# Cross-attention scores in four 32-row tiles of the array, with a new order of work on five engines

## What is computed

```python
q = (query @ Wq.T + bq).reshape(B, T, H, D).transpose(0, 2, 1, 3)
k = (key @ Wk.T + bk).reshape(B, S, H, D).transpose(0, 2, 1, 3)
v = (value @ Wv.T + bv).reshape(B, S, H, D).transpose(0, 2, 1, 3)
scores = jnp.einsum('bhtd,bhsd->bhts', q, k) * scale
scores = scores + attn_mask[None, None, :, :]
pad = key_padding_mask[:, None, None, :]
scores = jnp.where(pad, -jnp.inf, scores)
probs = jax.nn.softmax(scores, axis=-1)
out = jnp.einsum('bhts,bhsd->bhtd', probs, v)
out = out.transpose(0, 2, 1, 3).reshape(B, T, E)
return out @ Wo.T + bo
...
x = x + _L0_xattn_ref(_layernorm(x, axis=-1), ctx_1024, ctx_1024, ...)
```

## Time and profile before

| | |
|---|---|
| median of 3 runs | 3068.27 us (3065.03 to 3068.76) |
| profiled execution, its own time | 3058.43 us |
| its span | 3056.6 us |
| busy in the span: PE, PEld | 2634.9 us (86%), 2059.3 us (67%) |
| busy: DVE, ACT, POOL | 1635.3 us (54%), 1090.0 us (36%), 1049.3 us (34%) |
| mean granted TensorE clock | 0.886 of full speed |
| first cross-attention | from the start to about 850 us |

### The profile page before, as it was taken

One profiled execution on the slowest core, in us unless ns is written; L12 is line 12 of the kernel. 1 busy time (PEld: TensorE's weight loads), 2 busy tenths in 40 slices (PEclk: granted clock), 3 DMA queues, 4 the chain that ended last, 5 costly groups with the idle time before them and its releaser, 6 DMA issues. The chain is left out here.

```text
span 3056.6 us, 53637 instructions
## 1 busy us (share of the span) xinstructions
PE 2634.9 (86%) x15674; PEld 2059.3 (67%) x15687; DVE 1635.3 (54%) x5365; ACT 1090.0 (36%) x2422; POOL 1049.3 (34%) x1187
## 2 busy tenths in 40 slices
PE   4999999999969998529999999968879999957774
PEld 4999999999969997415555555546657888833332
DVE  3666666666646554652233333326555555557773
ACT  2555555555524442001112222211115555534442
POOL 3444555555300000227600000027744444313564
PEclk9999999999967776569999999985559999979996
DMA  3000000000070000135322222236640000000001
GB/s 136 22 21 21 21 21 21 21 21 21 1 262 1 0 0 10 52 131 192 137 68 76 77 77 77 78 125 221 225 147 1 0 0 0 0 28 1 1 0 55
DMA packets 110897, 180.88 MB, mean 59 GB/s; under 512 B 13665, under 2 KB 86370, under 8 KB 109410
## 3 DMA queue, kind: packets, MB, share of 16 engines
q1 hardware_dynamic: 75058, 114.79, 11.1%
q0 software_dynamic: 12288, 33.57, 3.0%
q10 hardware_dynamic: 23472, 31.54, 3.0%
HBM read 116.93 MB, written 62.91 MB: 59 GB/s over the span
## 5 line engine op out<-in xcount | busy, mean ns | idle before, releaser
L405 ACT ACTIVATE xa_prob<-xa_neg_s,xa_neg_max 128x256 f32<-128x256 f32 x512 | 232.9, 502 | 272.1 <-DVE xa_neg_max L298 272.1
L1618 PE MATMUL ex_ps_h<-moew_w,ex_xT 128*128 x576 | 286.2, 619 | 20.5 <-DVE ex_xT L1676 9.7
L254 POOL TENSOR_TENSOR xa_qz<-xa_q,g_head_mask 128x512 fp32r<-128x512 f32 x256 | 266.3, 1075 | 108.9 <-DVE xa_q L361 108.9
L298 DVE CUSTOM_DVE_ANT_0 xa_neg_s<-xa_ps_s,xa_mask 128x256 f32<-128x256 f32 x512 | 196.9, 422 | 174.8 <-PE xa_ps_s L445 173.9
L472 PEld LDWEIGHTS xa_ps_o<-xa_v,xa_probT 128*128 128x128 f32 x2048 | 259.4, 193 | 12.3 <-ACT xa_probT L412 3.9
L472 PE MATMUL xa_ps_o<-xa_v,xa_probT 128*128 128x34 f32 x2048 | 254.5, 269 | 1.7 <-ACT xa_probT L412 1.4
L445 PE MATMUL xa_ps_s<-xa_kT,xa_qz 128*128 128x256 f32 x1536 | 246.3, 296 | 1.8 <-POOL xa_qz L254 1.8
L1671 DVE TENSOR_TENSOR ex_g<-ex_act_g,ex_ps_h 128x256 f32<-128x256 f32 x144 | 60.7, 422 | 309.9 <-ACT ex_act_g L1651 309.9
L998 DVE CUSTOM_DVE_ANT_0 sa_neg_s<-sa_ps_s,sa_mask 128x128 f32<-128x128 f32 x512 | 117.8, 286 | 170.5 <-PE sa_ps_s L1114 170.1
L445 PEld LDWEIGHTS xa_ps_s<-xa_kT,xa_qz 128*128 128x128 f32 x1536 | 199.5, 190 | 2.0 <-issue 2.0
L412 ACT ACTIVATE xa_probT<-xa_ps_t 128x512 f32<-128x512 f32 x256 | 151.3, 591 | 138.9 <-PE xa_ps_t L456 138.7
(11 more groups left out here) (285 smaller groups left out, 5735.4 us busy)
## 6 DMA issues: line engine op xcount, KB each, us to landing
expert_rows<-sa_zero SPq DMA_DIRECT2D x12, 1536.0 KB, 14.5
ex_xg<-expert_rows SPq DMA_DIRECT2D x144, 128.0 KB, 2.0
expert_outs<-ex_y ACTq DMA_DIRECT2D x144, 128.0 KB, 1.7
xa_ctxT<-in_ctxT_dram SPq DMA_DIRECT2D x32, 512.0 KB, 3.4
xb_ctxT<-in_ctxT_dram SPq DMA_DIRECT2D x32, 512.0 KB, 4.9
xb_ctx_rows<-in_ctx_rows_dram SPq DMA_DIRECT2D x32, 512.0 KB, 3.6
moew_w<-in_moe_w_dram ACTq DMA_DIRECT2D x8, 1024.0 KB, 5.5
g_x<-in_x_dram SPq DMA_DIRECT2D x4, 1024.0 KB, 9.9
```

Source lines behind the costliest of these rows:

```text
L254: ins = nc.gpsimd.tensor_tensor(qz[:, pp, part, g, b, :].rearrange("p (h t) -> p h t", h=HG), q2[:, pp, part, g, b * T:(b + 1) * T].unsque ...
L298: ins = nc.vector.tensor_tensor_reduce(neg_s[:, u % 2, i, :], ps_s[u % 2][:, i * S:(i + 1) * S], mask[:, u // 4, :], -1.0, 3e38, ALU.add, ...
L405: ins = nc.scalar.activation(prob[:, u % 2, i, :], neg_s[:, u % 2, i, :], ACT.Exp, bias=neg_max[:, u % 2, i:i + 1], scale=-1.0)
L1618: mm = nc.tensor.matmul(ps_h[1 - par][:, :], xT[:, 1 - par, k, :], c.w1[:, own, k, :], start=(k == 0), stop=(k == KC - 1))
```

## The change

The scores of one batch are computed at once instead of in four units. A head pair has 32 rows of `q` and `k`, so the array is used as four tiles of 32 rows, one for each bank of `ps_s`, which has four banks now; `qz` needs only to keep the two heads of a pair apart (`in_pair`) and is half as large, four instructions of 128x256. The transposes go back into the banks of the scores. The mask is made on GpSimd, from a `pad` that is loaded tile by tile. The rounded keys are made on ACT (`high_keys`). And the order of the work in a step changes on PE, DVE, ACT and GpSimd.

```diff
-        pad = ph.sb("pad", [P, B, S], U8)
+        pad = ph.sb("pad", [P, 2, 2, S], U8)
...
-        ps_s = [ph.ps(f"s{i}") for i in range(2)]
-        ps_t = [ph.ps(f"t{i}") for i in range(2)]
+        ps_s = [ph.ps(f"s{j}") for j in range(4)]
...
-            sp.dma_start(pad[:, :, :], d["pad"].to_broadcast([P, B, S])).then_inc(mask_loaded, 16)
...
-                    wait(sp, ctx_low, s - 1)
+                    wait(sp, pad_ready, s - 1)
                     sp.dma_start(ctxT[:, par, :, :], d["ctxT"][s, :, :, :]).then_inc(ctx_loaded[par], 16)
+                    sp.dma_start(pad[:, par, :, :], d["pad"][s, :, :, :].to_broadcast([P, 2, S]))\
+                        .then_inc(pad_loaded[par], 16)
...
+            def masks(p, pp):
...
+                nc.gpsimd.tensor_scalar(pad_mask[:, :, :], pad[:, pp, :, :], MASKED, None, ALU.mult)                    .then_inc(pad_ready, 1)
+                pool.wait_ge(pad_ready, p + 1)
+                wait(pool, s_ready, 8 * p)
+                nc.gpsimd.tensor_tensor(mask[:, :, :], pad_mask[:, :, :],
+                                        attn[:, :].unsqueeze(1).to_broadcast([P, 2, S]), ALU.add).then_inc(mask_ready, 1)
+
             def step(s, par):
                 p, pp = s - 1, 1 - par
-                if live(p):
...
                 if live(s):
                     pool.wait_ge(ctx_high, s + 1)
                     wait(pool, v_done, 2 * (s - 1))
                     nc.gpsimd.tensor_tensor(ctx2[:, par, 1, :, :], ctxT[:, par, :, :], ctx2[:, par, 0, :, :],
                                             ALU.subtract).then_inc(ctx_low, 1)
                     ln.inverse_std(pool, nc, s, par)
+                if live(p):
+                    wait(pool, pv_done, 8 * (p - 1))
+                    nc.gpsimd.tensor_copy(v[:, pp, :, :, D:D1],
+                                          keep[:, p, :].unsqueeze(2).unsqueeze(3).to_broadcast([P, SC, H, 1]))\
+                        .then_inc(ones_ready, 1)
+
+                    pool.wait_ge(q_ready, p + 1)
+                    wait(pool, s_done, 8 * (p - 1))
+                    for part in range(2):
+                        for g in range(KC):
+                            ins = nc.gpsimd.tensor_tensor(
+                                qz[:, pp, part, g, :, :, :],
+                                q2[:, pp, part, g, :].rearrange("p (b t) -> p b t", b=2).unsqueeze(2)
+                                .to_broadcast([P, 2, 2, T]),
+                                in_pair[:, :].unsqueeze(1).unsqueeze(3).to_broadcast([P, 2, 2, T]), ALU.mult)
+                    ins.then_inc(qz_ready, 1)
+                    masks(p, pp)
...
+            def low_keys(p, pp, g):
+                dve.wait_ge(k_high, 2 * p + g + 1)
+                nc.vector.scalar_tensor_tensor(kT[:, pp, 1, g, :], (ps_b, ps_a)[g][:, :], bk[:, g:g + 1],
+                                               kT[:, pp, 0, g, :], ALU.add, ALU.subtract).then_inc(k_ready, 1)
...
+                    if u == 3 and live(p):
+                        low_keys(p, pp, 0)
+                        queries(p, pp)
...
+            def step(s, par):
+                p, a = s - 1, s - 2
+                for b in range(2):
+                    if b == 1 and live(p):
+                        high_keys(p, 1 - par, 1)
+                    for j in range(4):
+                        if live(a):
+                            probabilities(a, 4 * b + j)
+                        if j >= 1 and live(a):
+                            transposed(a, 4 * b + j - 1)
+                        if b == 0 and j == 3 and live(p):
+                            high_keys(p, 1 - par, 0)
                     if live(a):
...
+                        transposed(a, 4 * b + 3)
+                if live(s):
...
+                    nc.scalar.activation(ctx2[:, par, 0, :, :], ctxT[:, par, :, :], ACT.Copy).then_inc(ctx_high, 1)
...
+                if live(a - 1) or b:
+                    wait_apart(pe, t_ready, 8 * a + 4 * b, passed_pe)
+                for g in range(KC):
                     for n, (x, z) in enumerate(THREE_PASSES):
-                        mm = nc.tensor.matmul(ps_s[u % 2][:, i * S:(i + 1) * S],
-                                              qz[:, ap, x, g, b, j * P:(j + 1) * P],
-                                              kT[:, ap, z, g, b * S:(b + 1) * S], start=(n == 0), stop=(n == 2))
-                mm.then_inc(s_done, 1)
+                        for j in range(4):
+                            rows = slice(32 * j, 32 * (j + 1))
+                            mm = nc.tensor.matmul(ps_s[j][:, g * S:(g + 1) * S],
+                                                  qz[rows, ap, x, g, b, :, :].rearrange("p h t -> p (h t)"),
+                                                  kT[rows, ap, z, g, b * S:(b + 1) * S], start=(n == 0), stop=(n == 2))
+                            if g == KC - 1 and n == 2:
+                                mm.then_inc(s_done, 1)
```

More of the change, by code:

```diff
@@ new lines, in values @@
+            def values(p, pp, half):
+                dve.wait_ge(v_done, 2 * p + half + 1)
+                wait(dve, pv_done, 8 * (p - 1))
+                for i in range(2):
+                    ch = 2 * half + i
+                    ins = nc.vector.tensor_scalar(
+                        v[:, pp, ch, :, 0:D],
+                        (ps_a, ps_b)[half][:, i * E:(i + 1) * E].rearrange("p (h d) -> p h d", h=H),
+                        keep[:, p, ch:ch + 1], None, ALU.mult)
+                ins.then_inc(v_ready, 1)
@@ L433, in _, with scores @@
+            tile_steps(act, step, lag=2, peel=6)
         @block.tensor
         def _(pe):
-            def scores(a, u, ap):
-                b, g, jj = u // 4, u // 2 % 2, u % 2
-                if u == 0:
+            def scores(a, b, ap):
+                if b == 0:
                     pe.wait_ge(k_ready, 2 * a + 2)
                     pe.wait_ge(qz_ready, a + 1)
-                wait(pe, s_ready, 8 * a + u - 1)
-                for i in range(2):
-                    j = 2 * jj + i
+                if live(a - 1) or b:
+                    wait_apart(pe, t_ready, 8 * a + 4 * b, passed_pe)
+                for g in range(KC):
@@ new lines, in step @@
+                if live(a):
+                    scores(a, 0, ap)
+                if live(p):
+                    pe.wait_ge(ln.xn_ready, p + 1)
+                    wait(pe, v_ready, 2 * p - 1)
+                    wait(pe, yT_ready, 2 * p - 3)
+                    for k in range(KC):
+                        mm = nc.tensor.transpose(ps_a[:, k * P:(k + 1) * P], ln.xn[:, pp, k * P:(k + 1) * P],
+                                                 c.ident[:, :])
+                    mm.then_inc(xT_done, 1)
+                    keys(p, pp, 0)
@@ new lines, in step @@
+                if live(e):
+                    attended(e, 7, ep)
+                if live(a):
+                    transposes(a, 0)
+                if live(p):
+                    pe.wait_ge(xT_ready, p + 1)
+                    for g in range(KC):
+                        for k in range(KC):
+                            mm = nc.tensor.matmul(ps_a[:, g * P:(g + 1) * P], wq[:, k, g * P:(g + 1) * P],
+                                                  xT[:, pp, k, :], start=(k == 0), stop=(k == KC - 1))
+                    mm.then_inc(q_done, 1)
@@ new lines, in step @@
+                if live(a):
+                    attended(a, 2, ap)
+                if live(p):
+                    keys(p, pp, 1)
+                if live(a):
+                    scores(a, 1, ap)
+                    attended(a, 3, ap)
+                if live(e):
+                    pe.wait_ge(yT_ready, 2 * e + 2)
+                    for h2 in range(2):
+                        mm = nc.tensor.matmul(ps_b[:, 0:E], yT[:, ep, h2, :], wo[:, h2, :],
+                                              start=(h2 == 0), stop=(h2 == 1))
+                    mm.then_inc(o_done, 1)
```

293 lines of the change are left out of this document (128 added, 165 removed).

## The result

The changed kernel takes 3246.92 us (median of 4 runs, 3237.43 to 3259.22), the kernel before 3067.76 beside it (3065.03 to 3068.76, 4 runs): ratio 1.0588, 95% interval 1.0543 to 1.0633. It is 179 us slower, where 157 were predicted.

The account below looks back on a forecast made before the run. A ring of waits through four engines bounds the changed cross-attention: 28.9 us plus 2.0 for the clock make 30.9 a tile. With start and end the part ends at 1009, 159 us later: 3225 us, range 3130 to 3300.

Parts of the forecast that it names:

- The ring: First cross-attention: a closed chain of waits through PE, DVE, ACT and POOL sets the period, 28.9 us at full clock.
- link 1: POOL makes the mask behind qz, two instructions of 512 elements, PE's scores running under them: 2.1 us, upper end 2.8.
- signs of being wrong: Short PE wait before first scores, qz before unit 7's transposes, mask instructions much above 1 us, or clock staying 1.00.
- Link 3: ACT does four exponentials, three copies and the rounded keys: 6.0 us, taken as 5.6 because neighbours overlap.
- Link 4: DVE waits for the rounded keys, then makes their remaining part (0.75) and the queries (1.5): 2.3 us.
- link 5: PE waits for q_ready, then does keys (1.4) and the second scores (0.9): 2.3 us.
- link 6: PE without a gap: weighted sums, projection, values and transposes up to unit 7's: 7.8 us.
- links 9 and ones: POOL's subtraction and two layer norm instructions (3.2), then ones (0.3): 3.5 us.
- The clock: PE falls to 1.2 GHz after standing some 7 us each step: 2.0 us a tile on average, ends 0 and 5.
- Start: First scores at 38 instead of 45.72: 8 us from the pad transfer and the shorter qz together.
- End: After 30 intervals of 30.9: one interval of 22 without a new context, and about 22 for the last tile.
- The rival "ring open": An operand is made a tile earlier, so PE's work binds again: 22.4 us a tile, 2983 us; chance 5%.

Follow-up runs that it names:

- POOL's old order: Changed kernel with only POOL's order undone: ones, qz and masks ahead of the context's subtraction and layer norm; ratio 1.036 to the kernel before.
- mask ahead: Changed kernel with the uint8 half of the mask at the head of POOL's step instead of behind qz; ratio 1.0553 to the kernel before.
- filled wait: Changed kernel with 50 more 128x240 matmuls, whose results nobody reads, where PE waits behind a step's last heads; ratio 1.0597 to the kernel before.
- first open version: Changed kernel with ACT's context copy moved from the end of its step to the begin; ratio 0.9768 to the kernel before.

## Why the prediction was right, step by step

- **The ring** (the walk over ten links): shown. It vanishes when one of its links is moved, it is shorter by 3.4 with POOL's old order, and 1.27 us put in are paid with 3.4. Not every microsecond counts alone: 1.52 us taken out of link 1 gained nothing until the low clock was gone too. The profile's signs came as named: 76% PE, clock 0.84, 31 waits for `qz` with 205 us in sum, POOL's 21 us waits. So did one of the signs of being wrong: the uint8 instruction on POOL takes 1.52, where "much more than 1 us" was named.
- **Its length** is right by luck: two errors cancel, a link too short and a clock too dear. Measured on the turn shown: *link 1*, the mask, 3.35 instead of 2.1, beyond its upper bound of 2.8, since the uint8 input takes 1.52 for 512 elements a row and the plain sum 1.27, both above the 1.04 of `qz` that I took. *Link 2* 0.89 for 0.8. *Link 3* 6.15 for 5.6, with 0.63 of it a wait of ACT for transposes that PE at 1.2 GHz starts late. *Link 4* 2.1 for 2.3, *link 5* 2.5 for 2.3, *link 6* from 517.98 to where transposes 7 leave PE 8.1 for 7.8, *link 7* 0.9, *link 8* 1.05, *links 9 and ones* 3.3 for 3.5, *link 10* 2.4 for 2.5. They add to 30.7, for 28.9; the 0.63 of the clock is in them, so the ring at full clock is some 30.1.
- **The clock** was mis-sized the other way: 2.0 expected, about 0.7 paid (the 0.63 of link 3; and mask ahead plus filled wait take 2.2 from a full-clock step, 1.5 of it mask). The slow stretch at the step's head was foreseen, but I had not asked whether the mask covers it; the second fall, ahead of the second scores, came in no steady step (0.99). It came when the wait was filled.
- **Start**: 38 expected, 43.90 measured. The transfer gave 3.7 us (DVE's first instruction at 21.16 for 24.86) and not 6. The shorter `qz` gave nothing: it stands behind the low half of the second context from the first step on (37.96), and PE waited 2.99 for it. With POOL's old order first scores are at 41.33, in an execution whose DVE starts 1.0 sooner (20.20).
- **End**: the last interval and the last tile took 25.3 and 28.4 where I had 22 and 22, +9.7. Start (+5.9), end (+9.7) and 30 intervals (920 for 927) make 1017.6 for 1009.
- **The rival "ring open"**, 2983 at 22.4 a tile, was priced well: the first open version has 22.5 and, at the ratio, 2997 on the first chip. That PE works 20.4 in a step (20.5 measured) came out by luck: the tiles take off 3.6 and not the 4.5 of the sum, and 0.8 that the sum did not have comes from the rest of the change. The Trainium skill, page "TensorE: Matmul & The Clock Gate", section "Measured speedup vs the span model", has 3.07x for four row tiles; start to next start the groups here take 2.96 with full rows and 0.91 in tiles, 3.25x, and 2.6x if the 0.4 us that the neighbours of the two tiled groups lose is counted with them; the page's figure is for 512 columns, these move 256.

Not settled: why the low stretch in the middle comes in every second step of the first open version and not in the others, and what makes low stretches longer in some steps (the 3.4 paid for 1.27 hangs on it).

## What to carry to other kernels

When an order is rewritten, walk from the operand that a step starts with back through every queue it passes; if the walk comes to an instruction of the step before that stands last, the period is the length of that circle wherever it is longer than the busiest engine's work, and busy shares don't show it. One instruction then decides: here the same tiles are 5.6% slower or 2.3% faster by where a 1 us copy stands, and 4.3% faster with the next wait gone. A cost at nothing and a fix at nothing may be two covers over one another; try both together before giving up either.

## What the runs showed that I had not expected

- GpSimd takes 1.52 us for 128x512 from uint8 to f32, 1.27 for a sum of 128x512 in f32 and 0.61 for a product of 128x256.
- Groups of matmuls over all rows cost 0.06 to 0.11 us more each when they stand beside a group in 32-row tiles, 0.4 us a step here.
- Where PE's wait grew by 1.0 us (6.84 to 7.86), its slow stretch lasted from the end of the keys on to the queries; whether the wait did that is not shown. Filling the wait raised the mean clock from 0.83 to 0.94 and the kernel was no faster (1.0597 for 1.0562, with intervals that overlap, and an end of the part at 1048.4 for 1027.5), since the falls moved to where they are paid.
- One wait of PE of 0.77 us in a step of 21.7 stood between a clock that fell in about every second step and one that fell in none.
